# The first group's weight mixes spread over two groups, half of the row statistics moved behind the score rows, and one copy moved ahead of the exponential

## The reference, cut to what matters

```python
x = x + layernorm(attn(layernorm(x)))     # x: 4 batches x 2048 rows x 512
x = x + layernorm(ffn(layernorm(x)))
# attn: q, k, v = relu(x @ W + b); causal softmax(q k^T / sqrt(512)) @ v; relu(y @ Wo + bo)
# ffn: two gates (grouped product, batch norm, gelu, linear, softmax, top 32) around x @ weight
```

## Time and profile before

| | |
|---|---|
| median of 3 runs | 2080.33 us (2079.81 to 2081.18) |
| the profiled execution | 2080.73 us, its span 2078.9 us |
| TensorE busy | 1993.2 us, 96% |
| VectorE busy | 1609.5 us, 77% |
| ScalarE busy | 1157.2 us, 56% |
| GpSimd busy | 1203.1 us, 58% |

### The profile page before, as it was taken

One profiled execution on the slowest core, in us unless ns is written; L12 is line 12 of the kernel. 1 busy time (PEld: TensorE's weight loads), 2 busy tenths in 40 slices (PEclk: granted clock), 3 DMA queues, 4 the chain that ended last, 5 costly groups with the idle time before them and its releaser, 6 DMA issues.

```text
span 2078.9 us, 35448 instructions
## 1 busy us (share of the span) xinstructions
PE 1993.2 (96%) x11327; PEld 1128.1 (54%) x11327; DVE 1609.5 (77%) x3372; ACT 1157.2 (56%) x2568; POOL 1203.1 (58%) x1365
## 2 busy tenths in 40 slices
PE   7999999999999999999999999998999999999997
PEld 3666655566565566665557656544444444444443
DVE  8476766577676567766656855678999999999999
ACT  5445443355444336444335443334888888888885
POOL 6145351345534235444225452324999999999997
PEclk9999999999999999999999999999999999999999
DMA  7565765465675546656645564361223222222221
GB/s 239 150 164 142 177 144 153 100 167 155 177 168 141 132 122 165 154 161 151 147 121 152 154 147 135 108 165 56 76 87 103 96 87 97 87 92 96 98 77 66
DMA packets 350702, 270.64 MB, mean 130 GB/s; under 512 B 241970, under 2 KB 273842, under 8 KB 350516
## 3 DMA queue, kind: packets, MB, share of 16 engines
q1 hardware_dynamic: 331796, 205.71, 36.4%
q10 hardware_dynamic: 18720, 62.66, 10.4%
HBM read 145.34 MB, written 65.01 MB: 101 GB/s over the span
## 4 chain that ended last, share of the span: by engine, by line
PE 44%; DVE 18%; issue 13%; ACT 2%; DMA 0%; POOL 0%; DVEq 0%; ACTq 0%; POOLq 0%; SPq 0%
PE psum L812 29%; PE psum L866 6%; PE psum L838 6%; DVE c L1985 5%; DVE rest L1981 3%; DVE cut L1981 3%; DVE m L1969 2%; PE psum L1051 1%; DVE prod L1695 1%; DMA pT<-rows 0%; DVE dsq L1699 0%; DVE st L1549 0%; DVE hb L1688 0%; DVE rows L1656 0%; PE psum L958 0%
## 5 line engine op out<-in xcount | busy, mean ns | idle before, releaser
L812 PE MATMUL psum<-kT,qT 128*128 128x512 f16 (+3 forms) x1920 | 364.0, 347 | 5.7 <-DVE rows L1637 5.2
L812 PE MATMUL psum<-v,pT 128*128 128x512 f16 x1632 | 364.2, 380 | 2.0 <-DMA pT<-rows 2.0
L812 PEld LDWEIGHTS psum<-kT,qT 128*128 128x128 f16 x1920 | 180.8, 98 | 182.6 <-DVE rows L1637 6.7
L838 PE MATMUL psum<-hT_early,ring 128*128 128x256 f16 x2304 | 264.4, 275 | 13.9 <-ACT qT L1183 10.6
L812 PEld LDWEIGHTS psum<-v,pT 128*128 128x128 f16 x1632 | 159.9, 98 | 184.1 <-issue 5.0
L838 PEld LDWEIGHTS psum<-hT_early,ring 128*128 128x128 f16 x2304 | 227.2, 99 | 50.9 <-ACT qT L1183 11.4
L1985 DVE MAX8 c<-cut 128x8 f32<-128x512 f32 x384 | 244.2, 676 | 0.0
L1246 ACT ACTIVATE rows<-rows,nm 128x128 f32<-128x128 f32 (+7 forms) x64 | 76.9, 1201 | 226.4 <-DVE nm L1648 226.4
L812 PE MATMUL psum<-fw,h2T 128*128 128x512 f16 x768 | 177.0, 380 | 0.0
L812 PE MATMUL psum<-fw,xsT 128*128 128x512 f16 x768 | 176.2, 379 | 0.7 <-ACT xsT L1436 0.7
L2133 POOL TENSOR_SCALAR ve<-mv 128x1 f32<-128x1 f32 x64 | 23.0, 359 | 263.9 <-DVE mv L1674 263.2
(11 more groups left out here) (207 smaller groups left out, 4097.4 us busy)
## 6 DMA issues: line engine op xcount, KB each, us to landing
ring<-wc_scratch ACTq DMA_DIRECT2D x109, 512.0 KB, 4.5
xg<-x SPq DMA_DIRECT2D x64, 256.0 KB, 5.5
xr<-x SPq DMA_DIRECT2D x64, 256.0 KB, 3.4
h_scratch<-hb SPq DMA_DIRECT2D x64, 256.0 KB, 3.2
h<-h_scratch SPq DMA_DIRECT2D x64, 256.0 KB, 2.7
x<-x_scratch SPq DMA_DIRECT2D x64, 256.0 KB, 3.0
x_scratch<-xr SPq DMA_DIRECT2D x62, 256.0 KB, 2.3
out<-zn SPq DMA_DIRECT2D x59, 256.0 KB, 2.0
```

Of the source, the lines that this page charges most:

```text
L812: mm = nc.tensor.matmul(outp, stat(a), mov(c), start=(n == 0 and k == 0), stop=(n == total - 1 and k == 2))
L838: mm = nc.tensor.matmul(bank[:, 256 * m:256 * (m + 1)], ring[:, 2 * i + j, a, c, P * m:P * (m + 1)], hT_early[:, g % 2, 2 * j + t, b, c, : ...
```

## The change

Four edits. (1) The staging area's places are permuted (`STAGE`) so that q's and k's raw weights lie where the values of tiles 8 to 15 come, and can stay there longer; q's and k's mixed weights are split into two parts of `kT` that group 2 and group 3 fill. (2) The mixes move: v's from H = 0 to H = 2 on POOL, from H = 1 to H = 4 on ACT and DVE; q's and k's to H = 6 to 9 on POOL, to H = 8 and 10 on ACT and 9 and 11 on DVE. The stores of the plain weights (8 transfers a kind) go out in H = 1, 2, 3 and those of the mixed ones in H = 5, 10 and 15; DVE at H = 7 and ACT's first refill wait for the plain ones and v's mixed ones alone, and ACT waits for q's and k's stores before group 2 overwrites `kT`. (3) In groups after the first, `ln_stats` of tiles 2 and 3 leaves the end of h = 1 and is done in h = 2, behind `score_rows`. (4) In an opening's h = 2 and h = 4, ACT does `output` of o = 0 first and `exponential` after it.

```diff
+STAGE = (1, 3, 0, 2)
-                 "q": qT[:, 1], "k": kT[:, :, :, 512:1024]}
+                 "q": kT[:, :, :, 1024:1536], "k": kT[:, :, :, 1536:2048]}
...
@@ block.sync
+                def store_plain(kind):
+                    n = VQK.index(kind)
+                    sp.wait_ge(w_lo_ok.sem, w_lo_ok.at(1 + n))
+                    for p, (j, i) in enumerate(((0, 0), (1, 0), (0, 1), (1, 1))):
+                        for a in range(2):
+                            sp.dma_start(wc_d[n, :, p, 512 * a:512 * (a + 1)].rearrange("p (c n) -> p c n", c=2),
+                                         w_first[:, a, "qkv".index(kind), 2 * j:2 * j + 2, 256 * i:256 * (i + 1)]).then_inc(wc_out, 16)
...
-                    if H in (1, 3, 5):
-                        store_mixed(VQK[H // 2])
+                    if H in (1, 2, 3):
+                        store_plain(VQK[H - 1])
...
+                    if H in (5, 10):
+                        store_mixed(VQK[H // 5 - 1])
...
+                    if H == 15:
+                        store_mixed("k")
@@ block.scalar
+                    if (kind, g, o) == ("k", 2, 0):
+                        act.wait_ge(w_in[4], 16 + 32 * 8)
...
-                        act.wait_ge(wc_out, 32 * 8 * len(VQK))
+                        act.wait_ge(wc_out, 32 * 4 * (len(VQK) + 1))
...
-                            act.wait_ge(w_lo_ok.sem, w_lo_ok.at(4 + len(VQK)))
+                            act.wait_ge(w_lo_ok.sem, w_lo_ok.at(5))
...
-                        if h in (2, 4):
-                            exponential(s)
                         if h == 1:
                             s = s_tile(H - 1)
                         for o, span in ((2 * (h % 2), first), (2 * (h % 2) + 1, rest_of)):
                             output(kind, g, o)
+                            if h in (2, 4) and o == 0:
+                                exponential(s)
...
-                    if H in (1, 2, 4):
-                        mixed_hi(VQK[H // 2])
+                    if H in (4, 8, 10):
+                        mixed_hi({4: "v", 8: "q", 10: "k"}[H])
@@ block.vector
+                def rest_of_stats(g):
+                    if g < NG:
+                        for j in range(2, GROUP):
+                            ln_stats(g, j)
...
                     elif h in (2, 4) and kind and opening(g):
                         score_rows(s)
                         lo_output(kind, g, 0)
+                        if h == 2:
+                            rest_of_stats(g + 1)
...
                         score_rows(s)
                         if kind:
                             sum_11(kind, g)
+                        rest_of_stats(g + 1)
...
-                            dve.wait_ge(wc_out, 32 * 8 * len(VQK))
+                            dve.wait_ge(wc_out, 32 * 4 * (len(VQK) + 1))
...
-                    if H in (1, 2, 4):
-                        mixed_lo(VQK[H // 2])
+                    if H in (4, 9, 11):
+                        mixed_lo({4: "v", 9: "q", 11: "k"}[H])
...
                         if h == 1:
-                            for j in range(GROUP):
+                            for j in range(2 if g else GROUP):
                                 ln_stats(g + 1, j)
@@ block.gpsimd
-                    if H in (0, 1, 3):
-                        mix(VQK[(H + 1) // 2])
+                    if H == 2:
+                        mix("v", 0, 1)
+                    if H in (6, 7):
+                        mix("q", H - 6)
+                    if H in (8, 9):
+                        mix("k", H - 8)
```

More of the change, by code:

```diff
@@ L627, in transpose_h @@
                             .then_inc(hT_in[(0, 0, 1, 1, 2, 2, 3)[q]].sem, 16)
+                def store_plain(kind):
[5 more added lines that the diff above has]
+                                         w_first[:, a, "qkv".index(kind), 2 * j:2 * j + 2, 256 * i:256 * (i + 1)]).then_inc(wc_out, 16)
                 def store_mixed(kind):
                     n = VQK.index(kind)
-                    w = "qkv".index(kind)
                     sp.wait_ge(w_lo_ok.sem, w_lo_ok.at(5 + n))
-                    for p, whole, j, i in ((0, w_first[:, :, w], 0, 0), (1, w_first[:, :, w], 1, 0), (2, w_first[:, :, w], 0, 1),
-                                           (3, w_first[:, :, w], 1, 1), (4, mixed[kind], 1, 1), (5, mixed[kind], 0, 0),
-                                           (6, mixed[kind], 1, 0), (7, mixed[kind], 0, 1)):
+                    for p, (j, i) in enumerate(((1, 1), (0, 0), (1, 0), (0, 1)), 4):
                         for a in range(2):
                             sp.dma_start(wc_d[n, :, p, 512 * a:512 * (a + 1)].rearrange("p (c n) -> p c n", c=2),
-                                         whole[:, a, 2 * j:2 * j + 2, 256 * i:256 * (i + 1)]).then_inc(wc_out, 16)
+                                         mixed[kind][:, a, 2 * j:2 * j + 2, 256 * i:256 * (i + 1)]) \
+                                .then_inc(wc_out if kind == "v" else w_in[4], 16)
                 def first_ring():
@@ L716, in load_w @@
                     w, a, b = W_PIECES[n]
-                    sp.dma_start(w_stage[:, w, :, a:b], wqkvo[w].rearrange("(c p) n -> p c n", p=P)[:, :, a:b]).then_inc(w_in[n], 16)
+                    sp.dma_start(w_stage[:, STAGE[w], :, a:b], wqkvo[w].rearrange("(c p) n -> p c n", p=P)[:, :, a:b]).then_inc(w_in[n], 16)
                 load_x(0, 0)
@@ L1135, in weight_hi @@
                     dst = w_o[:, 0, :, a:b] if w == 3 else w_first[:, 0, w, :, a:b]
-                    nc.scalar.activation(dst, w_stage[:, w, :, a:b], ACT.Copy, scale=W_SCALE).then_inc(w_hi_ok.sem, 1)
+                    nc.scalar.activation(dst, w_stage[:, STAGE[w], :, a:b], ACT.Copy, scale=W_SCALE).then_inc(w_hi_ok.sem, 1)
                 def mixed_hi(kind):
                     act.wait_ge(mix_ok, 4 * (VQK.index(kind) + 1))
-                    nc.scalar.activation(mixed[kind][:, 0], w_stage[:, "qkv".index(kind)], ACT.Copy, scale=W_SCALE) \
+                    nc.scalar.activation(mixed[kind][:, 0], w_stage[:, STAGE["qkv".index(kind)]], ACT.Copy, scale=W_SCALE) \
                         .then_inc(w_hi_ok.sem, 1)
@@ L1536, in mixed_lo @@
                     dve.wait_ge(w_hi_ok.sem, w_hi_ok.at(5 + VQK.index(kind)))
-                    nc.vector.scalar_tensor_tensor(mixed[kind][:, 1], w_stage[:, "qkv".index(kind)], W_SCALE, mixed[kind][:, 0],
+                    nc.vector.scalar_tensor_tensor(mixed[kind][:, 1], w_stage[:, STAGE["qkv".index(kind)]], W_SCALE, mixed[kind][:, 0],
                                                    ALU.mult, ALU.subtract).then_inc(w_lo_ok.sem, 1)
```

22 lines of the change are left out of this document (12 added, 10 removed).

## The result

The changed kernel takes 2063.22 us (median of 4 runs, 2057.88 to 2066.54) against 2080.07 (4 runs, 2076.59 to 2081.18): a ratio of 0.9923, 95% interval 0.9903 to 0.9942, 16.9 us less. The forecast was 2053.8 with a range of 2046 to 2063. The direction is right, the gain is 9.6 us smaller than the 26.5 worked out. The profiled execution took 2064.47 us, its span 2062.7.

A forecast was written before the change was run, and what follows sets the result against it. The prediction took TensorE, busy 96% of the span, as the bound, leaving its idle time and what follows from it. Group 0's 11.0, the batches' 10.5 and the statistics' 5.0 made 26.5 us off 2080.33: 2053.8, range 2046 to 2063.

The forecast's parts named there:

- Group 0: Start of the kernel: moving the mixes shortens PE's stops and hides the wait for `hT_early`, 11.0 us gained (6 to 14).
- The moved mixes: q's and k's mixes, with ACT's and DVE's copies falling into group 1, were costed at nothing.
- a failing cover: Groups after group 0: without cover, k's mixed copy would hold back the next score rows by 2.3 to 3.4 us once.
- The statistics: Groups ahead of batch starts: two fewer statistics ahead of the score rows remove three PE waits, 5.0 us gained.
- The copy ahead of the exponential: Openings at batch starts: ACT copies the first output at once, PE's waits for `output` vanish, 10.5 us gained net.
- I take 3 x 1.1 = 3.3 as given back: Batch starts, groups 5, 9 and 13: PE, coming sooner, waits for DVE's last remainder of k, 3.3 us lost.
- The gross part: Batch starts: three vanished waits for `output`, 10.6 us, and the slow stretches behind them, 13.8 us in all.
- the bound of 9: Batch starts: upper bound, in us, on what the copy's gain gives back to waits for DVE; the lower was 0.
- Rival 3: Batch starts: DVE becomes the bound and asks the copy's gain back at h = 7; batches bring 3, 2061; chance 0.10.
- Rival 4: Batch starts: the copy did not hold PE, which waits there for something else; batches bring nothing, 2064; chance 0.04.
- Rival 2: Group 0 clogs at its new places, PE's gap ahead of `vo` 6 or 7 us; it brings 5, 2060; chance 0.16.
- rival 5: Every group: later statistics delay the transposes, 14 groups start waiting for `hT_early`, 46.6 us lost, 2100; chance 0.04.

The follow-up runs named there:

- e9: The changed kernel once more, unedited, timed and profiled again: 2061.73 us, ratio 0.991 to before.
- e5: The changed kernel with the copy's and the statistics' edits undone, so only the moved mixes are left: 2074.01 us, ratio 0.997 to before.
- e10: The changed kernel with all four row statistics ahead of the score rows again, second timing: 2065.07 us, ratio 0.9918 to before.
- e6: The changed kernel with all four row statistics ahead of the score rows again, first timing: 2064.24 us, ratio 0.9936 to before.
- e4: The changed kernel with h = 5's refill of the ring put behind `hi_vo` of h = 6 in openings: 2056.57 us, ratio 0.9894 to before.
- e3: The changed kernel with SP's two early transposes put behind the transpose of probabilities in openings: 2060.68 us, ratio 0.9915 to before.
- e1: The changed kernel with the copy's edit undone (exponential ahead of the first output in h = 2 and 4): 2069.08 us, ratio 0.9952 to before.
- e7: e4 with DVE's two last remainders of k ahead of half of the side work in an opening's h = 5: 2052.76 us, ratio 0.9872.
- e8: e7 with v's mixed weights split in H = 5 instead of H = 4: 2052.51 us, ratio 0.9868 to before.
- e12: e8 with SP's transpose of probabilities ahead of the early transposes in openings: 2049.94 us, ratio 0.9851 to before.
- e2: The changed kernel with the first copy ahead of the exponential in h = 2 alone: 2060.38 us, ratio 0.9914 to before.

## Why the prediction was wrong in size

**Group 0: right.** Forecast 11.0. To the end of group 1's first output the changed kernel gained 9.6 us in its first profile (78.16 to 68.54) and 12.1 in e9. The steps held one by one, within 1.3 us. The four norms beside v's mix:

```profile
35.95 5.72 DVE L1575 TENSOR_SCALAR xg<-xg,mv,rs 128x512 f32<-128x512 f32 x4 [0.93 <-POOL rs L2125]
```

That is 5.72 us, as the 5.71 of the earlier trace rows and three times the 1.91 of the earlier trace rows. It is what the Trainium skill's rule ("SBUF — State Buffer", Who interferes with whom) of a locked pair of ports makes of them, and the trace agrees. They end at 41.67, forecast 40.4; `vo` starts at 50.83, forecast 49.7, behind a gap of 3.42, forecast 3.8; the short gap ahead of k's last product was 1.74, forecast 1.0. The last transpose is issued at 56.95, and PE comes at 63.30 without a wait. Two things differ between the two profiles: the slow stretch behind `vo`'s gap, 1.4 us in the first and none in e9 for a forecast of 1.0, which was a matter of luck (below), and 1.0 us that was already lost when k's last product began (44.64 against 43.68).

**The moved mixes: small miss.** Costed at nothing, they cost 1.0 us at h = 7 of group 1 here, and 3.3 at h = 6 and 7 of it without the copy's edit (the expectation of e5 puts the 1.0 in group 2 and blames ACT's split of q's mixed weights; the rows shown above say otherwise). The prediction had priced a failing cover at 2.3 to 3.4, once, but at the next score rows. It failed later and through others: DVE, late by then, is seen by PE in `pT`, in k's last remainder and, through ACT, in `pilot`.

**The statistics: right where they stand.** Forecast 5.0, and 0.9 + 1.8 + 1.8 = 4.5 came in these columns (e10 against e9). But it is not kept: it is spent in the batch starts behind, 6.6 us in the three (e10 against e9), in the waits that the next step missed.

**The copy ahead of the exponential: the step that failed.** It is the sentence "I take 3 x 1.1 = 3.3 as given back". The gross part was right: the three waits for `output` went, with their slow stretch. Of its 13.8 us the batch starts should have kept 10.5; by the table they kept 4.0 in the first profile and 1.4 in e9, so that 10 to 12 were given back and not 3.3, more than the bound of 9. Not all of it is the copy's own: 6.6 are the statistics', as said, and with these undone the batch starts are 6.2 (e10) and 4.1 us (e6) shorter than with mixes alone.

The step asked only when DVE would be late, at h = 7, and missed the transfer that PE needs at h = 6. Before, `pT`'s transpose was issued 43.37 us after group 5's start and landed after 4.4, at 47.77, and PE took it up at 47.87: a cover of 0.1 us, which no wait in the list could show. After, PE was ready at 43.93, 3.94 sooner; the transpose was issued at 41.87, only 1.50 sooner, since ACT's exponential, DVE's `lo_p` and two transposes on SP stand ahead of it; and it took 5.8 to land, 1.4 longer. 3.94 - 1.50 + 1.4 - 0.1 = 3.7, and 3.92 was seen. In groups 9 and 13 the cover had been 2.1 and 1.6 us, and it went all the same: PE came 5.1 and 4.8 sooner, the issue 2.4 and 3.4, and the landing was 2.4 and 3.6 longer (6.3 and 6.6 for 3.9 and 3.0), which makes 3.0 and 3.4 for the 3.19 and 3.52 seen. There the longer landing is nearly all of it: without it 0.6 and nothing would have been left to wait. Some 2 us of it come with h = 5's refill (e4), which is issued 42.9 us into group 5 instead of 45.3, since PE frees the ring sooner; the rest is not shown.

To this comes the slow stretch, 1.3 to 1.7, in five of the six batch starts of the two profiles of this kernel: 4.06, 4.42, 4.34, 4.02 and 4.44 us in place of 2.75.

Rival 3 named the right kind of event and the wrong engine. Its mechanism is real, as e3 shows once the transfer is out of the way: DVE's k holds PE 2.6 to 2.7 us where 1.1 had been worked out. Its price, batches bringing 3, and its 2061 are near what came, but by way of the transfer and not of DVE: the changed kernel's own profiles show no wait for DVE's k. Rival 4 gave the batches nothing, and 2064: that is within a microsecond of the first timing, by luck (the second, 2061.73, is nearer to rival 3's), since its reason fails: the copy was what held PE, and the wait for something else stands some 20 us later, not at the same place. It had a chance of 0.04. Rival 2 (group 0 clogs) did not happen, and neither did rival 5: no group between begins with a wait for `hT_early`.

The ffn half was forecast unchanged and is, within its scatter.

## What to carry to other kernels

When an edit takes a wait from the bounding engine, every later input of that engine loses cover, those without any wait above all: for each of them, up to the next place with slack, subtract its landing from the engine's arrival and compare with how much sooner the chain that makes it starts. Transfers belong in this list, and they may get longer, since an engine that comes sooner also frees buffers sooner and so starts other transfers into them. Two bounds in a row hide each other: DVE's late remainder was worth nothing to remove while a transfer stood ahead of it, and some 4 us once that was shorter, so a null result of one edit doesn't clear its suspect.

## What the runs showed of the hardware

A gap of the same length does not always cost the clock. The stop ahead of `vo` in group 0 was 3.42 or 3.43 us in eleven profiles of kernels with the same code there; the 24 matmuls behind it took 5.35 in five of them (e1, e5, e6, e9, e10) and 6.75, 6.78, 7.04, 7.04, 8.04 and 8.24 in the others. The granted clock of the stretch was 0.78 in the first profile and 1.00 in e9. After gaps of 1.6 to 1.9 us it held (5.35 at 49.08 above). But behind 1.95 us in e1 24 matmuls took 4.35 instead of 2.79 (granted clock 0.62), behind 2.00 in group 14 of before 24 took 7.03 instead of 5.34 (0.76), and behind the 2.06 of e10 48 took 7.08 instead of 5.40 (0.76), while behind that kernel's 2.53 in group 13 12 took their 2.75. What decides it was not found.

A DMA transpose of one tile of probabilities landed 2.8 to 7.1 us after its issue, by what was under way: 2.8 to 2.9 ahead of the other transposes, 3.7 to 4.6 behind two of them with the refill moved away (e4, e7, e8), 5.8 to 7.0 behind two of them and with a refill of 512 KB issued 1 to 2 us later in the changed kernel. It isn't the whole rule: ahead of the others and without the refill it once took 3.7 (e12, group 5), in groups 9 and 13 of e1 and e2 3.0 to 3.1 with both, and in e10 and e5 5.9 with the refill 4.1 and 4.2 us behind. Which packets got in each other's way is open.
